# Attention scores of a fused attention and expert kernel: six bf16 products become three fp32r products in two row halves, with a new order for weight splits and scatters

## What is computed

```python
q = x @ wq_w.T + wq_b; k = x @ wk_w.T + wk_b; v = x @ wv_w.T + wv_b
q, k = _rope(q), _rope(k)                    # 16 heads of 16; 4 key heads, each for 4 query heads
att = einsum('bhqd,bhkd->bhqk', q, k) / 16 ** 0.5
att = softmax(where(tril, att, -inf))
x = layernorm(x + (att @ v) @ cp_w.T + cp_b)
weights, indices = top_k(sigmoid(x @ gate_w.T) + gate_b, 4); weights /= weights.sum(-1)
shared = (silu(x @ w1s) * (x @ w3s)) @ w2s
routed = sum over the 4 experts e of a token: weight_e * (silu((x @ w1[e]) * (x @ w3[e])) @ w2[e])
x = layernorm(x + shared + routed)
```

## Time and profile before

| | us |
|---|---|
| runs shown (3) | 693.66 to 699.48, median 697.44 |
| the profiled execution | 701.06 |
| its span | 699.3 |
| mean granted TensorE clock | 0.894 of full |

### The profile page before, as it was taken

The page is one execution under the profiler, slowest core; times in us unless marked ns, Lnnn a source line. Parts: engine busy times, 40 slices in busy tenths (PEclk is TensorE's granted clock), DMA queues, the critical chain, the costliest instruction groups (busy, mean ns, idle before and its releaser), DMA issues. The chain is left out here.

```text
span 699.3 us, 11914 instructions
## 1 busy us (share of the span) xinstructions
PE 561.5 (80%) x3708; PEld 363.4 (52%) x3708; DVE 454.6 (65%) x944; ACT 348.6 (50%) x759; POOL 307.3 (44%) x461
## 2 busy tenths in 40 slices
PE   4769987998899989589869877468999999999200
PEld 3434452443333544234323236458999999999100
DVE  4265537886775788578558116448777777776594
ACT  1216643566466557545555852235565666665022
POOL 3103324032743254836053731711677776776242
PEclk9959988899999999779798998869999999999655
DMA  4684614000511318212021232631344444441671
GB/s 117 114 186 68 98 42 63 6 25 1 132 40 40 47 43 156 73 40 94 1 74 58 65 88 62 203 97 47 98 136 126 126 128 120 130 131 36 240 300 60
DMA packets 53611, 64.92 MB, mean 93 GB/s; under 512 B 7995, under 2 KB 47310, under 8 KB 53552
## 3 DMA queue, kind: packets, MB, share of 16 engines
q1 hardware_dynamic: 46032, 46.45, 26.6%
q0 software_dynamic: 7104, 17.60, 7.1%
q10 hardware_dynamic: 416, 0.13, 0.1%
HBM read 32.49 MB, written 25.76 MB: 83 GB/s over the span
## 5 line engine op out<-in xcount | busy, mean ns | idle before, releaser
L1008 ACT ACTIVATE prob<-psT 128x512 f32<-128x512 f32 (+3 forms) x384 | 163.4, 496 | 107.3 <-PE psT L1521 101.8
L1230 DVE TENSOR_REDUCE MX<-psS 128x1 f32<-128x640 f32 (+6 forms) x176 | 175.7, 1027 | 47.5 <-PE psS L1556 45.3
L1552 PE MATMUL psS<-KS,QS 96*128 96x512 bf16 (+3 forms) x384 | 107.9, 362 | 18.9 <-DVE MX L1230 15.7
L1521 PE MATMUL psT<-QS,KS 98*128 98x512 bf16 (+3 forms) x384 | 106.5, 347 | 13.1 <-ACT prob L1008 8.2
L921 POOL TENSOR_SCALAR_AFFINE_SELECT prob<-prob 128x512 f32<-128x512 f32 x64 | 41.1, 643 | 139.9 <-ACT prob L1008 139.0
L973 POOL DMA_INDIRECT y_scratch<-ys,dst x80 | 80.9, 1011 | 37.8 <-POOL dst L966 18.7
L1536 PE MATMUL psO<-prob,V 128*32 128x512 f32 (+3 forms) x768 | 85.8, 521 | 8.9 <-POOL prob L921 7.2
L1726 PE MATMUL psH<-wU,xh 128*128 (+1 forms) x384 | 85.1, 345 | 9.3 <-issue 8.9
L892 POOL DMA_INDIRECT xs_scratch<-x1row,slotu x64 | 65.1, 1018 | 29.4 <-DVE slotu L1322 15.2
L1552 PEld LDWEIGHTS psS<-KS,QS 96*128 96x128 bf16 x384 | 34.1, 105 | 81.6 <-DVE MX L1230 46.8
L1726 PEld LDWEIGHTS psH<-wU,xh 128*128 128x128 f32 x384 | 65.3, 198 | 10.1 <-issue 10.1
(11 more groups left out here) (206 smaller groups left out, 983.3 us busy)
## 6 DMA issues: line engine op xcount, KB each, us to landing
xs<-xs_scratch SPq DMA_DIRECT2D x80, 134.0 KB
y<-y_scratch SPq DMA_DIRECT2D x8, 1024.0 KB, 12.3
QS<-qp SPq DMA_DIRECT2D x48, 128.0 KB, 4.6
wU_raw<-in_L_ffn_w_routed_dram SPq DMA_DIRECT2D x32, 176.0 KB, 3.4
xs_scratch<-padrow SPq DMA_DIRECT2D x1, 2144.0 KB
xs_scratch<-padrow SPq DMA_DIRECT2D x16, 134.0 KB
x1row<-in_L_attn_x_dram SPq DMA_DIRECT2D x4, 512.0 KB, 6.4
out_dram<-x1row SPq DMA_DIRECT2D x8, 256.0 KB, 2.1
```

What stands on the lines that cost most here:

```text
L1008: nc.scalar.activation(prob[:, step % NPROB, h, 0:HALF - c0], ps[:, 0:HALF - c0], ACT.Exp).then_inc(s_Tfree, 1)
L1230: nc.vector.tensor_reduce(out=MX[:, heads[0]:heads[-1] + 1, i - TH * q], in_=src, op=ALU.max, axis=AX_X).then_inc(s_Sfree, 1)
L1521: mm(ps[:, 0:HALF - c0], KS[b][:, g, j * P:(j + 1) * P], QS[:, QAT[(k // 2) % NSLOT], g % 2 * G + h, c0:HALF], start=True, stop=True).then ...
L1552: mm(ps[:, e * dist + c:e * dist + c + w], QS[0:ROWS, QAT[(k // 2) % NSLOT], g % 2 * G + h, (i - TH * q) * P:(i - TH * q + 1) * P], KS[b][ ...
```

## The change

- PAIRS has three entries: queries and keys are split into two fp32r parts, and hi x hi, lo x hi, hi x lo are summed. VectorE's remainder is part 1 itself; the ScalarE cast and the GpSimd subtraction ("split") are gone.
- A score needs 3 x 16 + 2 = 50 rows. Rows 0 to 63 and 64 to 127 hold two different heads' queries; the keys are stored in both halves. KS, QS, kp, qp, M2 and MT are four bytes wide. The two matmuls of a pair of heads stand behind each other, each in its row half.
- A kload or qload is still six DMAs (4 for part 0, 2 for part 1 or the reverse), of 64 rows with 2 KB each. KS's ones rows come by four DMAs (`ones_rows`) in place of two memsets (L1189). An mrow is two DMAs, one for each row half, in place of one.
- smax units with q = 1 are now 512 key columns or the rest of them for a pair of heads (16 units as before); the mask is added only where the unit holds the diagonal. VectorE joins the two maxima with one more instruction per group with q = 1.
- An "st" pair waits for the second last of the T ring before its first head, and the planner puts the two behind each other.
- `plan()` itself now puts in weight loads, splits and scatters: loads right after an evac, a split where ScalarE and GpSimd are ahead of TensorE and 5 us have passed since the load, a scatter where GpSimd is free.
- Memory is laid out anew: wA is loaded from group 8 on (before: groups 0 to 5), wU 1 and 2 at groups 2 and 4, and nine wU units come before the expert stage, eight (before: seven) in it, three of these in its first slot.

```diff
-PAIRS = ((0, 0), (0, 1), (0, 2), (1, 0), (1, 1), (2, 0))
+PAIRS = ((0, 0), (1, 0), (0, 1))
+SIDE = 64
+NS = P // SIDE
+NJ = G // NS
+QLOADS = len(PAIRS) * NS
...
-        return [(i, (h,), (i + 1) * P, 2 * HALF) for i in range(TH, TT) for h in range(G)]
+        return [(i, (j,), c, min((i + 1) * P - c, HALF)) for i in range(TH, TT) for j in range(NJ) for c in (0, HALF)]
...
-        return len(heads) * (n / 2400 + 0.06), 0, (len(heads) * n + 62) / 960 + extra
+        mask = 0.13 if i * P < c + n else 0
+        return len(js) * (n / 2400 + 0.03) + mask, 0, (NS * len(js) * n + 100) / 960 + extra
...
-        return (n / 2400, (n + 62) / 1200, 0) if kind == "st" else (4 * n / 2400 + 0.07, 0, 0)
+        return (n / 4800 + 0.02, (n + 80) / 1200, 0) if kind == "st" else (4 * n / 2400 + 0.07, 0, 0)
...
+def weight_units():
+    wA = [("wA", 3 * c, min(3 * c + 3, NX)) for c in range(6)]
+    wB = [("wB", 3 * c, min(3 * c + 3, NX)) for c in range(6)]
+    return {2: [("wU", 1)], 4: [("wU", 2)], 8: [("wU", 0)] + wA[0:2] + wB[0:1], 9: wA[2:4] + wB[1:2],
+            10: wA[4:6] + [("wU", 3)] + wB[2:3], 11: [("wU", 4), ("wU", 5)] + wB[3:4], 12: [("wU", 6)] + wB[4:5],
+            13: wB[5:6], 14: [("wU", 7), ("wU", 8)]}
...
+            if kind == "st" and item[3] % NS == 0:
+                at_ = max(at_, rings["T"][-2])
...
+    def behind(last):
+        while background and (background[0][0] == "wload" or last):
+            u = background.pop(0)[1:]
+            if u == ("wB", 0, 3):
+                clock["pool"] = max(clock["pool"], clock["pe"]) + 3.7
+                seq.append(("wzero",))
+            clock["sp"] = max(clock["sp"], clock["pe"]) + 1.3
+            seq.append(("wload",) + u)
+            splits.append((clock["sp"] + 5.0, u))
+        busy = clock["pe"]
+        if splits and (last or splits[0][0] <= busy and clock["act"] <= busy + 0.4 and clock["pool"] <= busy):
+            u = splits.pop(0)[1]
...
+            seq.append(("wsplit",) + u)
+        if scatters and (last or clock["pool"] <= busy):
+            seq.append(scatters.pop(0))
+            clock["pool"] = max(clock["pool"], busy) + 1.3
...
+        if item[0] == "st" and item[3] % NS == 0:
+            put(best[1].pop(0))
+        behind(False)
...
-LASTU = [("wU", s) for s in range(10, NX)]
+LASTU = [("wU", s) for s in range(9, NX)]
...
-LAST_AT = {0: LASTU[0:2], 1: LASTU[2:4], 3: LASTU[4:6], 4: LASTU[6:]}
+LAST_AT = {0: LASTU[0:3], 1: LASTU[3:5], 3: LASTU[5:7], 4: LASTU[7:]}
...
+                for n, pair in enumerate(PAIRS):
                     if pair[0] == part:
+                        for a in range(NS):
+                            row = a * SIDE + n * HD
+                            sp.dma_start(QS[row:row + HD, QAT[s % NSLOT], :, :].bitcast(F32),
+                                         qp[a * SIDE:(a + 1) * SIDE, m, part, q * HALF:(q + 1) * HALF].bitcast(F32)
+                                         ).then_inc(s_qload[s % NSLOT], 16)
...
-                    nc.vector.scalar_tensor_tensor(out=rest[0:rows, n % NREST, :], in0=ps[0:rows, 0:HALF], scalar=bias,
-                                                   in1=part[:, 0, :], op0=ALU.add, op1=ALU.subtract).then_inc(s_Sfree, 1)
+                    nc.vector.scalar_tensor_tensor(out=part[:, 1, :], in0=ps[0:rows, 0:HALF], scalar=bias,
+                                                   in1=part[:, 0, :].bitcast(F32), op0=ALU.add,
+                                                   op1=ALU.subtract).then_inc(s_part2, 1)
...
-                    if T_NO[item] > 3:
+                    if kind == "st":
+
+                        if item[3] % NS == 0 and T_NO[item] > 2:
+                            pe.wait_ge(s_Tfree, T_NO[item] - 2)
+                    elif T_NO[item] > 3:
                         pe.wait_ge(s_Tfree, T_NO[item] - 3)
...
-                    mm(ps[:, 0:HALF - c0], KS[b][:, g, j * P:(j + 1) * P],
-                       QS[:, QAT[(k // 2) % NSLOT], g % 2 * G + h, c0:HALF], start=True, stop=True).then_inc(s_T, 1)
+                    rows = slice(h % NS * SIDE, h % NS * SIDE + QROWS)
+                    mm(ps[:, 0:HALF - c0], KS[b][rows, g, j * P:(j + 1) * P],
+                       QS[rows, QAT[(k // 2) % NSLOT], g % 2 * NJ + h // NS, c0:HALF], start=True, stop=True).then_inc(s_T, 1)
...
+                    for e, j in enumerate(js):
+                        for a in range(NS):
+                            rows = slice(a * SIDE, a * SIDE + ROWS)
+                            last = mm(ps[:, a * HALF + e * w:a * HALF + (e + 1) * w],
+                                      QS[rows, QAT[(k // 2) % NSLOT], g % 2 * NJ + j, (i - TH * q) * P:(i - TH * q + 1) * P],
+                                      KS[b][rows, g, c:c + w], start=True, stop=not diag)
+                        for a in range(NS if diag else 0):
+                            d = a * HALF + e * w + i * P - c
+                            last = mm(ps[:, d:d + P], ident_b[:, :], mask_b[:, :], start=False, stop=True)
```

More of the change, by code:

```diff
@@ L254, in put @@
         end += HOP
[L255 to L257 removed]
+        if kind == "cp":
             clock["pool"] = end = max(clock["pool"], end) + 0.65
@@ L288, in plan @@
         ahead += [("smax", k, n) for n in range(len(max_units(HEADGROUPS[k][1])))] + [("mrow", k)]
-    splits = [("split",) + i[1:] for i in ahead if i[0] == "proj"]
     evacs = [("evac", k) for k in range(NK)]
@@ L295, in plan @@
             norms += rows_items(b, q) if k < NK - 1 else []
-    streams = [splits, loads, evacs, ahead, pvs, norms, exps]
+    streams = [loads, evacs, ahead, pvs, norms, exps]
     while any(streams):
@@ L762, in run @@
                     _, b, half = item
-                    for part in range(3):
+                    for part in range(2):
                         keys_part(b, half, part)
```

253 lines of the change are left out of this document (116 added, 137 removed).

## The result

The changed kernel takes 777.95 us (median of 4 runs, 770.34 to 797.4) against 697.88 us of the kernel before in the same session: a ratio of 1.112, 95% interval 1.102 to 1.122. The prediction was 682 us, with 709 as the upper end; the sign was wrong, and the time is outside the range. A few executions of one and the same kernel were slower than the rest at a lower granted clock (797.4 us here, at 0.73; 838.67 and 928.26 us of the kernel before in the session of e13 to e16, at 0.63 and 0.56), and the ratios leave them out.

What follows compares the result with a forecast made beforehand. It took attention to be bound by a circle of waits, an in-order TensorE feeding two rings with no engine full. Terms summed to -15.5 on 701.06, giving 685.6, scaled 682 us; range 652 to 709.

Steps and rivals of the forecast that it cites:

- TensorE's 11 us: Attention's score products: net TensorE saving from pairing heads after paying for mask changes, 12 to 13 at clock 0.9.
- Clock: Rival: TensorE in attention gets 1.2 GHz more often, 10 us per further tenth, scaled 688; chance inside the other cases.
- I take 0.11: Masked smax pairs: each change between row halves and full array costs 0.11 us, in either direction.
- The slower rival: Attention: masked pairs drain the array twice, and halves run one after the other or drains cost double; 708 us, chance 0.18.
- A pair's own cost: Attention's score pairs: two four-byte weight loads one after the other make each pair cost 0.22 us at any width.
- halves in full: Rival: in attention, halves' loads overlap and changes are nearly free, TensorE 62 us less; 657 us, chance 0.18.
- Half of TensorE's saving counts: Attention: TensorE's saving counts only where it is the late engine, put at half, giving -6 us.
- The splits' places: Attention: planner places splits singly where ScalarE is ahead, avoiding bursts; -9 us, bounds 0 and -18.
- The first scores: Start of attention: the first qload ends about 0.6 us earlier.
- The gate on pairs: Score pairs in the last group: the new gate nearly eats the -2.5 us gain, up to 0.2 us per step.
- Casts, joined maxima and the second mrow DMA: Small terms: removed casts and subtractions -2 us, joining maxima on VectorE +1, second DMA of an mrow +1.
- The sign test I had set: Forecast wrong if attention ends before 380 or after 412 us; unchanged attention at lower clock means gain went into clock.

Runs made afterwards that it cites:

- e13: Kernel before with the changed kernel's planner placing weight loads, splits and scatters, old weight schedule kept: 671.5 us, ratio 0.966.
- e16: Kernel before with score rows filled with zeros, no masks in the maxima and the planner's places: 663.5 us, ratio 0.954.
- e5: Kernel before without masks in the maxima and with three of its six bf16 products, so 50 rows: 767.7 us, ratio 1.101.
- e6: Kernel before without masks in the maxima and with five of its six bf16 products, so 82 rows: 714.1 us, ratio 1.020.
- e11: Changed kernel with the pairs' rows filled with zeros to 64 per half, masks kept: 735.3 us, ratio 1.049.
- e7: Changed kernel with every pair of products issued twice, the second over the first: 805.0 us, ratio 1.154.
- e18: e16 with a two-column product in a row half ahead of each of the 96 score steps: 681.1 us, ratio 0.971.
- e12: Changed kernel with each mask product contracted over its own head's 64 rows only: 735.4 us, ratio 1.050.
- e3: Changed kernel with weight splits and scatters placed by the kernel before's rule: 773.5 us, ratio 1.118.
- e17: Changed kernel, zero-filled and without masks in the maxima, with the old gate on the scores' banks: 702.4 us, ratio 1.000.
- e4: Kernel before without the 256 mask products in the row maxima: 691.5 us, ratio 0.995.
- e2: Changed kernel with both heads of a pair taken from row half 0, one after the other: 881.3 us, ratio 1.269.

## Why the prediction was wrong, point by point

- **The step that failed** is the clock. The sum converted TensorE's 11 us "at the mean clock of 0.9", as if the change left the clock where it was, and the rival called "Clock" priced a further tenth of attention at 1.2 GHz at 10 us and had no chance of its own. Attention's clock fell from 0.90 to 0.69, which is four tenths more of it at 1.2 GHz. The price was too low as well: filling rows with zeros alone, with every instruction of TensorE kept, gave back two tenths (0.69 to 0.80) and was worth 43 us, by this estimate 20 us a tenth. My reading of the stage table ("TensorE with less to do gets 1.2 GHz more often") had the direction; what I didn't draw from it is that a pair is at work for half the time of two products, and with 100 rows. Rows alone (e5, e6, e11) and time alone (e7) each moved the clock that way.
- **The changes** were the second step that failed. "I take 0.11" held for the way into the full array (0.10) and failed for the way back into two four-byte halves (0.20 at full clock, 0.30 at half). In e18 a change into a half with one two-byte product cost 0.10, so a change by itself is not the 0.20; what the rest is, weights or width of the operands, was not tested. The changes around the masks were worth 43 us (e12), where my term had 28 us of changes at half their value.
- **The slower rival** had the right sign and part of the mechanism. It put the point of loss at 0.16 us per change, and the mean of both ways is 0.15; but its halves one after the other did not happen, and by the prices at full clock TensorE would still have gained. Its 708 us came nearest to the result and had no clock in it.
- **A pair's own cost** (0.22 at any width) held at 512 columns (0.24) and was wrong the other way at 128 (0.06). The misreading is in the earlier trace rows: fp32r products of 256 columns that come every 0.11 us are just streaming (256 / 2400 = 0.107) and show no load that isn't hidden, and the 0.11 between products of 16 columns did not carry over to the pairs. The first rival, "halves in full", was right about the halves, wrong about free changes, and its 657 us was the furthest from the result. The streaming saved was real and was not worth having.
- **A slip in the "Clock" rival.** 10 us on the forecast of 685.6 is about 695, and scaled about 692; the text's 691.5 is already scaled, and 688 is scaled twice.
- **Half of TensorE's saving counts** rested on a TensorE that was late half of the time. In the changed kernel it was late more often: ScalarE's wait for it grew from 101.8 to 174.4 us.
- **The splits' places**: -9 with -18 as the far bound, measured -22 to -24 in the kernel before (e13) and nothing in the changed one (e3). The sum's terms were not independent: this one seems to need a TensorE that is not the late engine.
- **Small terms.** The first scores came later, not 0.6 us earlier: maxima start at 36.0 instead of 33.6. The gate on pairs, a doubt of mine, costs nothing that shows (e17). Casts, joined maxima and the second mrow DMA were not tried alone; VectorE's and ScalarE's busy time in attention moved by 2 us each.
- **The sign test I had set** (wrong if attention ends after 412; a lower clock as the sign that the gain went into the clock) pointed at the right row of the profile: attention ended at 485.9, at 0.69.

## What to carry to other kernels

Where TensorE's clock is not at full in the stage that is edited, an edit that gives the array less to do is not a saving until the granted clock of the stage is priced: look at how many rows are at work and for how long, before and after, and not at TensorE's busy time alone. Spare rows of a contraction are worth trying to fill, with zeros if need be: here that gave 43 us in the halves, 2.4% in the kernel before without masks, and nothing that shows in the kernel before with them. Row halves beside whole-array products in one stream cost 0.3 us per round trip here, more than the 0.21 us that pairing two products of 512 columns saves, so keep one shape per stage or leave the halves alone.

## What the runs showed of the hardware that I had not expected

- With fewer rows at work the granted clock was lower at about the same busy time or more: 98, 82 and 50 rows over the same columns gave 0.87, 0.81 and 0.68 in attention (e4, e6, e5), and a stretch of e2 with TensorE busy 66.86 of 67.5 us, its scores on 48 to 50 rows, stayed at 1.2 GHz.
- Rows of zeros count: 50 to 64 rows per half raised attention's clock from 0.69 to 0.80 (e11).
- Two row halves with four-byte weights cost about what one product costs: a pair of 512 columns ends 0.24 us after the pair before it, one of 128 columns 0.06.
- A change of shape is not one price: 0.10 us from a pair into the full array, 0.20 back into a pair of four-byte halves, 0.30 at 1.2 GHz, 0.10 into a single two-byte half and 0.11 out of it.
